# A hybrid Mamba, expert, attention and windowed-transformer layer on one core: GpSimd's difference in two halves, one clip over two PSUM banks, and other due times for the planner

## The chip, the cores and the metric

One core of a Trainium2 chip runs the whole program. The time is that of one execution on the device, in microseconds (us); a timing is the median of several runs. Engines are called as in the profile: PE (TensorE, with PEld for its weight loads), DVE (VectorE), ACT (ScalarE), POOL (GpSimd) and SP (SyncE, which issues DMAs). On-chip memory is SBUF; the results of matmuls land in PSUM, eight banks of 512 float32 for each of 128 partitions.

## The reference

The input x has 16 sequences of 256 tokens with 128 features, all in float32. Two blocks follow one another, and each adds two branches to its input:

```python
xn = layernorm(x)
x = x + mamba(xn) + experts(xn)            # selective scan, 256 channels, 16 states; top-1 of 8 experts, 512 hidden
xn = layernorm(x)
x = x + all_token_attention(xn) + windowed_transformer(xn)
```

The all-token attention has 16 heads of 8 features. Its weights are a power of an angle:

```python
q, k = l2norm(q), l2norm(k)
cos = einsum("bhsd,bhtd->bhst", q, k)
g = arccos(clip(cos, -1 + 1e-7, 1 - 1e-7))
score = (1 + g) ** (-3.2)
n_r, n_c = score.sum(-1), score.sum(-2)
k_tilde = score / n_r / n_c
probs = k_tilde / max(k_tilde.sum(-1), 1e-12)
out = (probs @ v) @ w_out.T + b_out
```

The windowed transformer has two layers of 8 heads of 64 features, each with normed and rotated queries and keys, a window of 64 tokens, and a gated feed-forward of width 341.

## The kernel before

The 16 sequences are worked in 8 pairs of 512 tokens. The work is cut into units, named by a letter and a step: `e_*` are the experts, `m_*` the Mamba branch of a pair (16 steps of a scan over 128x1024 elements), `f_*` the sum of the first block and the second layernorm, `g_*` the all-token attention, and `shift`, `qkv`, `heads`, `score` and so on the windowed layers. The branches of one pair depend on each other (attention of pair n needs `m_out` of pair n), but the scan of pair n+1 can overlap with the attention of pair n.

**The all-token attention of a pair** (`g_*`) has 8 blocks, one for each sequence b and four heads. For each block, m in the code:

1. `g_score`: twice, for two heads each, PE writes the cosines into two PSUM banks (L984), and DVE clips them into `cl`, one instruction of 128x512 for each bank (L1506). `cl` is a single buffer of 4 heads; DVE waits for the difference of the block before (`g_sub`), and each clip counts up `v_gs`.
2. `g_ln`: ACT writes ln(1 + c) into `la` (L1255) and ln(1 - c) over `cl` (L1257). 
3. `g_sub`: POOL forms the difference `la - cl` of 128x2048 elements in one instruction (L1726).
4. `g_tan`: Tanh (L1263) and Arctan (L1266), which give the angle; `g_pow`: Ln and Exp (L1273, L1275), which give the score.
5. `g_av`: DVE sums a block's columns (L1513) and scales the values, PE multiplies; `g_ev`, `g_avT`, `g_oT` and `g_out` finish; L1544 adds the attention of a pair to its input, L1549 the windowed layers.

`la` has two buffers, so two blocks are on their way together. ACT's functions lie in different tables, and a change of table is an instruction of its own (L758).

**Other work that the rows name.** A scan step is a product (L1428), a scan (L1434) and a product (L1440) on DVE, all of 128x1024 in SBUF; PE sums the states (L942); L1446 multiplies by the gate, at a pair's end. In the windowed layers POOL adds the rotated halves of queries and keys, 128x1024 (L1730); DVE takes a maximum over the sums of squares (L1572), scales by the norms (L1577), reduces scores over two banks for the softmax (L1587, L1588), and scales the output out of PSUM (L1601).

**The order.** A planner, run when the kernel is built, fixes the order of each engine's queue and the PSUM banks. `all_units` gives each unit a due time (`want`) and what it comes after; `schedule` walks through time, and each engine that is free takes the ready stage with the smallest due time, plus `SWITCH` if ACT would have to change its table. `STAGES` holds what a stage is taken to cost. Due times are a regular pattern (`EARLY`, `FIRST`, `SECOND`, `PERIOD`: the attention of pair i starts at EARLY + PERIOD x i, the Mamba branch of pair n from 2 on at FIRST + SECOND + 60 + PERIOD x (n - 2), and its step k stands 18 + k x (PERIOD - 30)/16 later), plus an offset for each kind of unit (`LATER`). On the chip each queue runs in that order, and semaphores hold an instruction until its inputs are there:

```python
cost = want[unit] + (SWITCH if needs and needs != table else 0)
if best is None or cost < best[0]:
    best = (cost, x, needs)
```

A unit that takes two banks got any two idle ones, except `score` of the windowed layers, whose two are neighbours, so that one instruction can read both.

## Time and profile before

| | |
|---|---|
| median of 3 runs | 2499.11 us (2494.23 to 2502.01) |
| the profiled execution | 2502.13 us, span 2500.8 us |
| busy in the span: PE, DVE, ACT, POOL | 1993.4, 1930.0, 1833.5, 525.0 us |
| mean granted clock of PE | 0.842 of full speed |
| instructions: PE, DVE, ACT, POOL | 10866, 3005, 2759, 206 |

The span runs from the first to the last instruction of the profiled execution; its time on the device is 1.3 us longer. Busy time is the sum of an engine's instructions; an instruction that is held up while it runs counts as busy for that long. The rows further down give groups of instructions (line, engine, operation, output and inputs, count), with their busy time, the mean of one in ns, and the idle time of the engine before them, with what ended it.

### The profile page before, as it was taken

To read this page: it belongs to the slowest core of one execution; us is meant where nothing else is said; L and a number is where in the kernel's file an instruction comes from. 1 tells how busy PE (TensorE), PEld (TensorE's weight loads), DVE (VectorE), ACT (ScalarE), POOL (GpSimd) and SP (SyncE) were. 2 spreads that over 40 slices of the span, in tenths; PEclk is the share of its full clock that TensorE was granted. 3 is DMA by queue.
4 is the path that set the end of the run, shared out by engine and by line. 5 is a ranking of instruction groups with operands and counts; after the bars stand their busy time and mean duration, and the time that the engine had idled before them with its cause. 6 is when DMAs were issued, how large, how long until landed. Compare 5 with 4: busy or idle time off the path is not lost.

```text
span 2500.8 us, 32678 instructions
## 1 busy us (share of the span) xinstructions
PE 1993.4 (80%) x10866; PEld 1328.3 (53%) x10866; DVE 1930.0 (77%) x3005; ACT 1833.5 (73%) x2759; POOL 525.0 (21%) x206
## 2 busy tenths in 40 slices
PE   4777778888678878878787888878787878888867
PEld 2544546775345555655465555655455555655645
DVE  5788895545997889699867889699968889674554
ACT  3436868697669677887777787887678786978883
POOL 2413121022112121302212121302112211221220
PEclk8787878999887888888787989888687989776778
DMA  7631112432211110111001110111001010000000
GB/s 250 222 98 56 51 34 67 131 116 85 83 42 53 46 35 18 40 35 55 22 13 48 39 48 13 40 46 53 13 31 39 32 53 1 1 1 5 1 1 5
DMA packets 67527, 126.29 MB, mean 51 GB/s; under 512 B 8836, under 2 KB 40132, under 8 KB 67236
## 3 DMA queue, kind: packets, MB, share of 16 engines
q1 hardware_dynamic: 61808, 113.19, 13.9%
q0 software_dynamic: 2816, 7.21, 0.8%
q10 hardware_dynamic: 2740, 3.80, 0.4%
q8 instruction: 92, 1.51, 0.2%
q14 instruction: 71, 0.58, 0.1%
HBM read 111.33 MB, written 12.85 MB: 50 GB/s over the span
## 4 chain that ended last, share of the span: by engine, by line
PE 31%; DVE 30%; ACT 18%; issue 16%; DMA 2%; SPq 1%; POOL 1%; DVEq 0%; ACTq 0%; POOLq 0%
PE ps L763 6%; DVE hB L1434 5%; PE ps L984 4%; PE ps L942 4%; DVE hB L1428 3%; DVE hB L1440 2%; PE ps L1068 2%; ACT arena L1255 2%; ACT arena L1331 2%; PE ps L1043 2%; DVE arena L1506 2%; DVE n_c L1513 2%; ACT L758 2%; PE ps L1103 2%; DVE lss L1568 2%
## 5 line engine op out<-in xcount | busy, mean ns | idle before, releaser
L1726 POOL TENSOR_TENSOR arena<-arena 128x2048 f32<-128x2048 f32 x64 | 297.5, 4649 | 1188.9 <-ACT arena L1257 1188.8
L763 PE MATMUL ps<-w_ident,arena 128*128 128x128 f32 x1647 | 301.1, 319 | 123.6 <-ACT arena L1331 43.7
L942 PE MATMUL ps<-hB,w_ident 128*128 128x512 f32 x512 | 303.4, 725 | 75.3 <-DVE hB L1440 75.2
L763 PEld LDWEIGHTS ps<-w_ident,arena 128*128 128x128 f32 x1647 | 227.7, 166 | 234.1 <-issue 139.1
L1434 DVE TENSOR_TENSOR_SCAN hB<-dA,hB 128x1024 f32<-128x1024 f32 x128 | 324.6, 2539 | 9.1 <-ACT dA L1219 8.8
L1730 POOL TENSOR_TENSOR arena<-arena,rb 128x1024 f32<-128x1024 f32 x64 | 151.9, 2374 | 574.6 <-DVE rb L1566 574.6
L1219 ACT ACTIVATE dA<-dtv,w_A_log 128x510 f32<-128x510 f32 x256 | 168.8, 718 | 109.6 <-DVE hB L1434 108.6
L1043 PE MATMUL ps<-w_l_wqkv,arena 128*128 128x512 f32 x384 | 212.5, 677 | 33.7 <-DVE lss L1568 15.5
L1506 DVE TENSOR_SCALAR arena<-ps 128x512 f32<-128x512 f32 x256 | 163.8, 681 | 63.6 <-PE ps L984 62.8
L1331 ACT ACTIVATE arena<-ps,nmx 128x128 f32<-128x128 f32 (+1 forms) x512 | 158.9, 397 | 65.5 <-DVE nmx L1588 64.8
L942 PEld LDWEIGHTS ps<-hB,w_ident 128*128 128x128 f32 x512 | 106.3, 229 | 181.9 <-issue 116.2
L1428 DVE TENSOR_TENSOR hB<-BC,du 128x1024 f32<-128x1024 f32 x128 | 180.4, 1414 | 28.6 <-PE ps L942 24.2
L984 PE MATMUL ps<-gqT,gkT 8*128 8x256 f32 x1024 | 176.3, 469 | 31.2 <-issue 12.4
L758 ACT ACT_TABLE_LOAD x142 | 182.2, 1283 | 15.3 <-issue 12.8
L1440 DVE TENSOR_TENSOR hB<-hB,BC 128x1024 f32<-128x1024 f32 x128 | 188.6, 1476 | 0.6
L1513 DVE TENSOR_REDUCE n_c<-arena 128x8 f32<-128x2048 f32 x64 | 145.8, 2278 | 31.6 <-ACT arena L1275 31.4
L1338 ACT ACTIVATE PT<-ps 128x384 f32<-128x384 f32 x256 | 124.3, 487 | 59.1 <-PE ps L763 42.3
L1255 ACT ACTIVATE arena<-arena,one_b 128x2048 f32<-128x2048 f32 x64 | 128.3, 2004 | 53.2 <-DVE arena L1506 45.2
L984 PEld LDWEIGHTS ps<-gqT,gkT 8*128 8x128 f32 x1024 | 106.5, 218 | 93.0 <-issue 81.2
L1068 PE MATMUL ps<-arena 64*128 64x128 f32 (+1 forms) x1024 | 154.9, 383 | 0.0
L1087 PEld LDWEIGHTS ps<-arena,PT 128*128 128x128 f32 x512 | 93.3, 218 | 113.7 <-ACT PT L1338 57.2
L1087 PE MATMUL ps<-arena,PT 128*128 128x65 f32 x512 | 107.2, 295 | 52.4 <-ACT PT L1338 43.9
(198 smaller groups left out, 4216.3 us busy)
## 6 DMA issues: line engine op xcount, KB each, us to landing
BC<-bc_d SPq DMA_DIRECT2D x128, 512.0 KB, 3.7
BC<-in_experts SPq DMA_DIRECT2D x31, 514.0 KB, 3.3
arena<-in_experts SPq DMA_DIRECT2D x15, 514.0 KB, 3.6
arena<-in_x SPq DMA_DIRECT2D x8, 256.0 KB, 5.8
xnT_d<-arena SPq DMA_DIRECT2D x8, 256.0 KB, 3.7
hB<-xnT_d SPq DMA_DIRECT2D x8, 256.0 KB, 2.6
x<-in_x SPq DMA_DIRECT2D x8, 256.0 KB, 2.9
out<-go SPq DMA_DIRECT2D x8, 256.0 KB, 2.3
```

The costliest lines, as they stand in the source:

```text
L758: a.preload_act_table_set(names[0])
L763: return t.transpose(out_, in_, ident[0:k, 0:k])
L942: e = t.matmul(lb(), ident, hB[k % 2][:, j], start=q == 0 and j == 0, stop=q == NQ - 1 and j == NG - 1)
L984: e = t.matmul(lb(z)[:, kt * L:(kt + 1) * L], gkT[32 * hi:32 * hi + GD, hb, kt * P:(kt + 1) * P], gqT[32 * hi:32 * hi + GD, hb], start=Tru ...
L1043: t.matmul(lb(), hT1[b][:, tt * P:(tt + 1) * P], w_lqkv[:, l, w * INNER:(w + 1) * INNER], start=True, stop=True).then_inc(p_q[b], 1)
L1068: e = t.matmul(o_, q_, kT[head_rows(z), k, b * L + j0:b * L + (L if qt else P)], start=False, stop=True)
L1331: e = a.activation(sm[b][:, hh, at], lb(z)[:, cols], ACT.Exp, bias=nmx[b][:, qt, hh:hh + 1])
L1428: v.tensor_tensor(hB[k % 2], Bb[q % 2], bc(du[:, c:c + 1], [P, NG, T]), ALU.mult).then_inc(v_bx, 1)
L1434: v.tensor_tensor_scan(hf, flat2(dA[k % 2]), hf, 0.0, ALU.mult, ALU.add).then_inc(v_scan, 1)
L1440: v.tensor_tensor(hB[k % 2], hB[k % 2], Cb[q % 2], ALU.mult).then_inc(v_hc, 1)
L1506: v.tensor_scalar(cl[:, 2 * (k % 2) + z], lb(z), -1.0 + 1e-7, 1.0 - 1e-7, ALU.max, ALU.min).then_inc(v_gs, 1)
L1726: g.tensor_tensor(la[m % 2], la[m % 2], cl, ALU.subtract).then_inc(g_sub, 1)
```

## The change

It has three parts.

- **The clip.** `g_score` takes two neighbouring banks, and one DVE instruction clips both, 128x1024 elements. It waits for the one half of the difference before it that reads the same part of `cl`; `v_gs` counts once for two banks.
- **The difference.** `g_sub` becomes two units a block, each one instruction on two heads (128x1024), each with a signal. Tanh waits for both halves; the next block's first pair of heads waits for the first half only.
- **The plan.** In the planner the clip is taken as 1.2 instead of 1.3, a difference as 2.4 instead of 4.6; `SWITCH`, `LATER` and the four numbers of the pattern have other values, and a new table, `STREAM`, shifts the due times of a whole branch of one pair. So each engine's queue has another order.

```diff
--- before.py
+++ after.py
@@ -64,8 +64,8 @@
     "m_fin": [("DVE", 1.5)], "x_load": [("SP", 0.1)], "m_out": [("PE", 2.1), ("DVE", 0.62)],
     "f_yg": [("POOL", 4.0)], "f_ln": [("DVE", 2.9), ("ACT", 0.6)], "f_xn": [("DVE", 1.1)], "f_tr": [("PE", 0.6), ("DVE", 0.7)],
     "g_qkv": [("PE", 0.86), ("DVE", 0.5)], "g_sq": [("ACT", 1.05), ("DVE", 1.5)], "g_norm": [("ACT", 0.7)],
-    "g_hd": [("DVE", 0.4), ("PE", 0.6), ("ACT", 0.5)], "g_score": [("PE", 1.3), ("DVE", 1.3)], "g_ln": [("ACT", 3.9)],
-    "g_sub": [("POOL", 4.6)], "g_tan": [("ACT", 3.8)], "g_pow": [("ACT", 3.9)], "g_av": [("DVE", 2.9), ("PE", 1.1)],
+    "g_hd": [("DVE", 0.4), ("PE", 0.6), ("ACT", 0.5)], "g_score": [("PE", 1.3), ("DVE", 1.2)], "g_ln": [("ACT", 3.9)],
+    "g_sub": [("POOL", 2.4)], "g_tan": [("ACT", 3.8)], "g_pow": [("ACT", 3.9)], "g_av": [("DVE", 2.9), ("PE", 1.1)],
     "g_ev": [("ACT", 0.5)], "g_avT": [("PE", 0.6), ("DVE", 1.15)], "g_oT": [("PE", 0.6), ("ACT", 0.5)],
     "g_out": [("PE", 1.2), ("DVE", 0.65)], "out": [("DVE", 0.65), ("SP", 0.1)], "zeros": [("DVE", 0.3)],
     "shift": [("PE", 0.4), ("ACT", 0.8)], "norm": [("DVE", 0.2), ("ACT", 0.5)], "qn": [("DVE", 1.25)], "heads": [("PE", 1.2), ("ACT", 1.0)],
@@ -79,14 +79,16 @@
 
 NEEDS = {"e_ln": "ln", "e_route": "ln", "m_weights": "ln", "m_dt": "ln", "m_ex": "ln", "f_ln": "ln", "g_norm": "ln", "g_ln": "ln", "g_pow": "ln",
          "norm": "ln", "score": "ln", "ln": "ln", "m_in": "silu", "g_tan": "tan", "gelu": "gelu"}
-SWITCH = 67.0
-
-LATER = {"down": 6, "f_ln": -5, "f_tr": 21, "f_xn": -15, "f_yg": -29, "g_av": 20, "g_avT": -6, "g_ev": 2, "g_hd": -38,
-         "g_ln": -22, "g_norm": -40, "g_oT": -1, "g_out": -13, "g_pow": 49, "g_score": -4, "g_sq": -18, "g_sub": -49,
-         "gelu": 57, "heads": 39, "hid": 4, "l_weights": 22, "ln": -31, "ln2": 29, "lnT": -27, "m_B": 56, "m_C": -54,
-         "m_bx": -16, "m_dt": 2, "m_du": -36, "m_ex": -7, "m_fin": 28, "m_hc": 8, "m_in": -88, "m_load": -3, "m_out": 20,
-         "m_scan": 21, "m_sum": -28, "m_weights": -1, "m_xp": -13, "norm": -31, "oT": 17, "on": 3, "out": -36, "pt": -3,
-         "pv": 54, "qkv": -6, "score": 3, "shift": 16, "wo": -9, "x_load": 18, "zeros": 50}
+SWITCH = 78.0
+
+LATER = {"down": 13, "f_ln": 28, "f_tr": -33, "f_xn": -25, "f_yg": 146, "g_av": 1, "g_ev": 10, "g_hd": -89, "g_ln": -13,
+         "g_norm": 26, "g_out": -5, "g_pow": 17, "g_qkv": -28, "g_score": -56, "g_sq": -4, "g_sub": 14, "g_tan": 6,
+         "gelu": -25, "hid": 10, "l_weights": -31, "ln": 41, "ln2": 11, "lnT": -84, "m_B": 132, "m_C": 11, "m_bx": 3,
+         "m_dt": 16, "m_du": -5, "m_ex": 53, "m_fin": 86, "m_hc": 136, "m_in": -23, "m_load": 14, "m_out": 5, "m_scan": -2,
+         "m_weights": -67, "m_xp": 29, "norm": -3, "on": 20, "out": -3, "pv": 13, "qkv": -4, "qn": -8, "score": -1, "up": 7,
+         "wo": 8, "x_load": 55, "zeros": -12}
+
+STREAM = {("g", 0): 1, ("g", 6): 1, ("g", 7): -8, ("l", 6): 1, ("l", 7): -7, ("m", 5): 2}
 
 LOADED = [15.0, 24.0]
 
@@ -111,13 +113,20 @@
     return STAGES[u]
 
 
+def stream(unit):
+    u, n, b, k = unit
+    if u in [x for x, _ in LAYER]:
+        return "l", n // LAY
+    return ("-" if u == "m_weights" else u[0][0]), n
+
+
 def all_units():
 
     want, after = {}, {}
 
     def unit(time, what, *comes_after):
         what = what + (0,) * (4 - len(what))
-        want[what] = time + LATER.get(what[0], 0.0)
+        want[what] = time + LATER.get(what[0], 0.0) + STREAM.get(stream(what), 0.0)
         after[what] = [x + (0,) * (4 - len(x)) for x in comes_after]
 
     for n in range(NPAIR):
@@ -182,7 +191,7 @@
              *[("f_tr", i - 2) for z in range(1) if i >= 2])
         unit(start - 20, ("f_ln", i), ("f_yg", i), ("m_out", i))
         unit(start - 20, ("f_xn", i), ("f_ln", i))
-        unit(start - 20, ("f_tr", i), ("f_xn", i), *[("g_sub", i - 1, 1, HB - 1) for z in range(1) if i])
+        unit(start - 20, ("f_tr", i), ("f_xn", i), *[("g_sub", i - 1, 1, 2 * HB - 2 + z) for z in range(2) if i])
         for tt in range(TT):
             unit(start, ("g_qkv", i, 0, tt), ("f_tr", i))
         unit(start, ("g_sq", i), *[("g_qkv", i, 0, tt) for tt in range(TT)])
@@ -198,14 +207,18 @@
                 t1 = start + 2 * cycle * b + cycle * (hb // 2)
                 z = hb % 2
                 m = HB * b + hb
-                prev = [("g_sub", i, *divmod(m - 1, HB))] if m else [("g_sub", i - 1, 1, HB - 1)] if i else []
+
+                p_ = (i, *divmod(m - 1, HB)) if m else (i - 1, 1, HB - 1)
+                prev = [[("g_sub", p_[0], p_[1], 2 * p_[2] + y)] if p_[0] >= 0 else [] for y in range(2)]
+                subs = [("g_sub", i, b, 2 * hb + y) for y in range(2)]
                 prev2 = [("g_av", i, *divmod(m - 2, HB))] if m >= 2 else [("g_av", i - 1, 1, HB - 2 + m)] if i else []
-                unit(t1, ("g_score", i, b, 2 * hb), *[("g_hd", i, b, k) for k in range(4)], *prev)
-                unit(t1, ("g_score", i, b, 2 * hb + 1), ("g_score", i, b, 2 * hb), *prev)
+                unit(t1, ("g_score", i, b, 2 * hb), *[("g_hd", i, b, k) for k in range(4)], *prev[0])
+                unit(t1, ("g_score", i, b, 2 * hb + 1), ("g_score", i, b, 2 * hb), *prev[1])
                 unit(t1, ("g_ln", i, b, hb), ("g_score", i, b, 2 * hb), ("g_score", i, b, 2 * hb + 1), *prev2)
-                unit(t1, ("g_sub", i, b, hb), ("g_ln", i, b, hb))
-
-                unit(t1 + 12, ("g_tan", i, b, hb), ("g_sub", i, b, hb), *[("g_sub", i, b, hb + 1) for x in range(1) if z == 0])
+                for y in range(2):
+                    unit(t1, subs[y], ("g_ln", i, b, hb))
+
+                unit(t1 + 12, ("g_tan", i, b, hb), *subs, *[("g_sub", i, b, 2 * hb + 3) for x in range(1) if z == 0])
                 unit(t1 + 20, ("g_pow", i, b, hb), ("g_tan", i, b, hb), *[("g_tan", i, b, hb + 1) for x in range(1) if z == 0])
                 unit(t1 + 20, ("g_av", i, b, hb), ("g_pow", i, b, hb), *prev2, *[("g_av", i, b, hb - 1) for x in range(1) if hb],
                      *[("g_ev", i, *divmod(m // 2 - 1, 2)) for x in range(1) if z == 0 and m], *[("g_ev", i - 1, 1, 1) for x in range(1) if m == 0 and i])
@@ -265,7 +278,7 @@
     return want, after
 
 
-EARLY, FIRST, SECOND, PERIOD = 49.0, 120.0, 105.0, 239.0
+EARLY, FIRST, SECOND, PERIOD = 120.0, 130.0, 80.0, 230.0
 
 
 def landed(unit):
@@ -370,7 +383,7 @@
 
     def choose(unit, count):
 
-        if unit[0] != "score":
+        if unit[0] not in ("score", "g_score"):
             return sorted(idle[0:count]) if len(idle) >= count else None
         pairs = [[z, z + 1] for z in range(7) if z in idle and z + 1 in idle]
         return min(pairs, key=lambda x: max(idle.index(z) for z in x)) if pairs else None
@@ -783,6 +796,10 @@
         def bank(unit, m=0):
             return ps[:, plan["banks"][bank_of(unit)][m]]
 
+        def two_banks(unit):
+            z0, z1 = plan["banks"][unit]
+            return ps[:, z0:z1 + 1:z1 - z0]
+
         before = shared_before(plan)
         all_first, all_wm, all_w = 16 * len(first), 16 * len(mamba), 16 * len(later)
 
@@ -985,7 +1002,7 @@
                                          gqT[32 * hi:32 * hi + GD, hb], start=True, stop=True)
                     e.then_inc(p_gs, 1)
                     for z in range(2):
-                        read_by(unit, v_gs, HB * m + 2 * (k % 2) + z + 1, z)
+                        read_by(unit, v_gs, 2 * m + k % 2 + 1, z)
                 elif u == "g_av":
                     m = BLOCKS * i + HB * b + k
                     if k % 2 == 0:
@@ -1248,7 +1265,7 @@
                     m = BLOCKS * i + HB * b + k
                     at, c_ = la[m % 2], cl
                     use(LN_EXP)
-                    a.wait_ge(v_gs, HB * (m + 1))
+                    a.wait_ge(v_gs, 2 * (m + 1))
                     if m >= 2:
                         a.wait_ge(p_av, m - 1)
                         a.wait_ge(v_vt, m - 1)
@@ -1259,7 +1276,7 @@
                     m = BLOCKS * i + HB * b + k
                     at = la[m % 2]
                     use(SIG, GELU, SILU)
-                    a.wait_ge(g_sub, m + 1)
+                    a.wait_ge(g_sub, 2 * (m + 1))
                     a.activation(at, at, ACT.Tanh, scale=0.25).then_inc(a_own, na.up())
                     use(SIG)
                     a.wait_ge(a_own, na.n)
@@ -1472,7 +1489,7 @@
                 elif u == "f_tr":
                     v.wait_ge(p_xT, i + 1)
                     if i:
-                        v.wait_ge(g_sub, BLOCKS * i)
+                        v.wait_ge(g_sub, 2 * BLOCKS * i)
                     v.tensor_copy(xnT, lb()).then_inc(v_xT, 1)
 
                 elif u == "g_qkv":
@@ -1500,10 +1517,10 @@
                 elif u == "g_score":
                     m, hb = BLOCKS * i + HB * b + k // 2, k // 2
                     if m:
-                        v.wait_ge(g_sub, m)
+                        v.wait_ge(g_sub, 2 * (m - 1) + k % 2 + 1)
                     v.wait_ge(p_gs, 2 * m + k % 2 + 1)
-                    for z in range(2):
-                        v.tensor_scalar(cl[:, 2 * (k % 2) + z], lb(z), -1.0 + 1e-7, 1.0 - 1e-7, ALU.max, ALU.min).then_inc(v_gs, 1)
+                    v.tensor_scalar(cl[:, 2 * (k % 2):2 * (k % 2) + 2], two_banks(unit), -1.0 + 1e-7, 1.0 - 1e-7,
+                                    ALU.max, ALU.min).then_inc(v_gs, 1)
                 elif u == "g_av":
                     m = BLOCKS * i + HB * b + k
                     hs = slice(k * HB, (k + 1) * HB)
@@ -1582,8 +1599,7 @@
                     if 4 * n + k >= 2:
                         v.wait_ge(a_e[b], 4 * n + k - 1)
                     hs = slice(2 * (k % 2), 2 * (k % 2) + 2)
-                    z0, z1 = plan["banks"][unit]
-                    both = ps[:, z0:z1 + 1:z1 - z0]
+                    both = two_banks(unit)
                     v.tensor_reduce(nmx[b][:, 0, hs], both[:, :, 0:P], AX.X, ALU.max, negate=True)
                     v.tensor_reduce(nmx[b][:, 1, hs], both[:, :, P:SC], AX.X, ALU.max, negate=True).then_inc(v_mx[b], 1)
                 elif u == "on":
@@ -1721,9 +1737,10 @@
                     for tt in range(TT):
                         g.indirect_dma_start(xn[i % 2][:, tt], None, y_d[q], bass.IndirectOffsetOnAxis(slot[:, TT * i + tt:TT * i + tt + 1], 0)).then_inc(d_yg[i % 2], 16)
                 elif u == "g_sub":
-                    m = BLOCKS * i + HB * b + k
+                    m = BLOCKS * i + HB * b + k // 2
+                    half = slice(2 * (k % 2), 2 * (k % 2) + 2)
                     g.wait_ge(a_ln, m + 1)
-                    g.tensor_tensor(la[m % 2], la[m % 2], cl, ALU.subtract).then_inc(g_sub, 1)
+                    g.tensor_tensor(la[m % 2][:, half], la[m % 2][:, half], cl[:, half], ALU.subtract).then_inc(g_sub, 1)
                 elif u == "qkv" and k % 3 == 1:
                     tt = 2 * b + k // 3
                     g.wait_ge(v_rot[b], 2 * (2 * n + k // 3 + 1))
```

## Rows read from the trace of the kernel before

**Rows 1.** The page: busy time and span share; the chain by engine and line.

```profile
PE 1993.4 (80%) x10866; PEld 1328.3 (53%) x10866; DVE 1930.0 (77%) x3005; ACT 1833.5 (73%) x2759; POOL 525.0 (21%) x206
...
PE 31%; DVE 30%; ACT 18%; issue 16%; DMA 2%; SPq 1%; POOL 1%; DVEq 0%; ACTq 0%; POOLq 0%
PE ps L763 6%; DVE hB L1434 5%; PE ps L984 4%; PE ps L942 4%; DVE hB L1428 3%; DVE hB L1440 2%; PE ps L1068 2%; ACT arena L1255 2%; ACT arena L1331 2%; PE ps L1043 2%; DVE arena L1506 2%; DVE n_c L1513 2%; ACT L758 2%; PE ps L1103 2%; DVE lss L1568 2%
```

**Rows 2.** Stretches: PE, PEld, DVE, ACT, POOL busy (instructions), clock, DMA share, GB/s.

```profile
625.00:2115.00 1490.00, 1206.21 (x6444) 778.12 (x6443) 1279.91 (x1830) 1144.25 (x1636) 301.08 (x101) 0.85 0.11 38
2115.00:2500.00 385.00, 311.75 (x1807) 223.11 (x1805) 214.99 (x429) 283.93 (x402) 79.25 (x24) 0.79 0.01 2
```

**Rows 3.** Groups of instructions on POOL: busy us, mean ns | idle before.

```profile
L1726 POOL TENSOR_TENSOR arena<-arena 128x2048 f32<-128x2048 f32 x64 | 297.5, 4649 | 1188.9 <-ACT arena L1257 1188.8
...
L1730 POOL TENSOR_TENSOR arena<-arena,rb 128x1024 f32<-128x1024 f32 x64 | 151.9, 2374 | 574.6 <-DVE rb L1566 574.6
```

**Rows 4.** Groups of instructions on DVE, same columns.

```profile
L1434 DVE TENSOR_TENSOR_SCAN hB<-dA,hB 128x1024 f32<-128x1024 f32 x128 | 324.6, 2539 | 9.1 <-ACT dA L1219 8.8
...
L1440 DVE TENSOR_TENSOR hB<-hB,BC 128x1024 f32<-128x1024 f32 x128 | 188.6, 1476 | 0.6
...
L1446 DVE TENSOR_TENSOR xs<-xs,zs 128x512 f32<-128x512 f32 x16 | 29.7, 1856 | 0.6
```

**Rows 5.** Single lines: duration ns min/median/max, first and last start us.

```profile
L1434 DVE TENSOR_TENSOR_SCAN hB<-dA,hB x128: 2258/2282/6550, 68.5 to 2099.7; 128x1024 f32<-128x1024 f32 x128
...
L1440 DVE TENSOR_TENSOR hB<-hB,BC x128: 1192/1217/5564, 76.5 to 2102.6; 128x1024 f32<-128x1024 f32 x128
...
L1446 DVE TENSOR_TENSOR xs<-xs,zs x16: 691/693/4844, 161.7 to 2112.0; 128x512 f32<-128x512 f32 x16
...
L1506 DVE TENSOR_SCALAR arena<-ps x256: 658/680/693, 206.5 to 2404.0; 128x512 f32<-128x512 f32 x128
```

**Rows 6.** Timeline of POOL and DVE: start us, us, instruction.

```profile
845.33 4.51 POOL L1726 TENSOR_TENSOR arena<-arena 128x2048 f32<-128x2048 f32 x1 [35.34 <-ACT arena L1257]
...
845.44 5.48 DVE L1440 TENSOR_TENSOR hB<-hB,BC 128x1024 f32<-128x1024 f32 x1
...
850.84 1.21 DVE L1428 TENSOR_TENSOR hB<-BC,du 128x1024 f32<-128x1024 f32 x1
...
997.05 0.56 DVE L1601 TENSOR_TENSOR arena<-ps,rs 128x384 f32<-128x384 f32 x1
```

**Rows 7.** Timeline of POOL: first and last of 40 differences that hold up DVE.

```profile
218.72 5.32 POOL L1726 TENSOR_TENSOR arena<-arena 128x2048 f32<-128x2048 f32 x1 [1.64 <-ACT arena L1257]
...
2390.39 4.50 POOL L1726 TENSOR_TENSOR arena<-arena 128x2048 f32<-128x2048 f32 x1 [4.79 <-ACT arena L1257]
```

**Rows 8.** Chain that ended last: first and last of 45 held-up pieces.

```profile
219.59 4.50 DVE lss L1572
...
2390.73 5.25 DVE arena L1577
```

**Rows 9.** Groups on DVE: the clips and the reductions over two banks.

```profile
L1506 DVE TENSOR_SCALAR arena<-ps 128x512 f32<-128x512 f32 x256 | 163.8, 681 | 63.6 <-PE ps L984 62.8 <-POOL arena L1726 0.4 <-issue 0.2
...
L1588 DVE TENSOR_REDUCE nmx<-ps 128x2 f32<-128x384 f32 x128 | 70.0, 547 | 0.0
...
L1587 DVE TENSOR_REDUCE nmx<-ps 128x2 f32<-128x256 f32 x128 | 53.4, 417 | 78.4 <-PE ps L1068 78.1
```

**Rows 10.** Waits for the clips: us in total, times, longest us.

```profile
ACT arena L1255 <- DVE arena L1506: 45.2, 28, 4.7
...
PE ps L984 <- DVE arena L1506: 11.8, 10, 2.4
```

**Rows 11.** Timeline of DVE: the attention results of pairs 4 to 6.

```profile
1682.80 0.68 DVE L1544 TENSOR_TENSOR go<-ps,x 128x512 f32<-128x512 f32 x1
...
1980.09 0.66 DVE L1544 TENSOR_TENSOR go<-ps,x 128x512 f32<-128x512 f32 x1
...
2224.64 0.69 DVE L1544 TENSOR_TENSOR go<-ps,x 128x512 f32<-128x512 f32 x1
```

## The prediction

> **What bounds the kernel now.** I read the page first: busy shares and the composition of the chain that ended last, then the stages, then single groups of instructions. The reader is to see that no engine is full: TensorE is busy for 80% of the span, VectorE for 77%, ScalarE for 73%, GpSimd for 21%, and the chain is shared by TensorE (31%), VectorE (30%), ScalarE (18%) and issue (16%) [rows 1]. So the order in which the three queues meet sets the time, and a microsecond taken from one engine gives back a part of itself. The stages differ [rows 2]: from 625 to 2115 us, where scans and attention overlap, VectorE is busy for 1280 of 1490 us (86%); from 2115 us to the end no scan runs and it falls to 56%. GpSimd's long instruction is the difference of the logarithms, 64 times 4.65 us [rows 3].
>
> The rows then show something that no share shows. VectorE's scan takes 2282 ns in the median, but 2539 in the mean and 6550 at most; the multiplication behind it 1217 and 1476, the product with the gate 693 and 1856 [rows 4, 5]. The timeline says when: the long ones overlap GpSimd. At 845.33 GpSimd begins a difference of 4.51 us, at 845.44 VectorE begins a multiplication that takes 5.48 us instead of 1.22, and ends 1.1 us after GpSimd [rows 6]. I matched every VectorE instruction that is over 0.15 us above its group's median with the GpSimd instruction running then: 40 of the 64 differences hold up a VectorE instruction (the first at 218.72, the last at 2390.39 us [rows 7]), 123 us together, and 31 of the 64 rotary additions hold one up for 47 us more; 170 us in all. Held up are instructions with two inputs in SBUF, and a few with one, as the maximum over the sums of squares at 219.59 [rows 8]; the clips, which read PSUM, stay between 658 and 693 ns [rows 5]. Where those instructions stand in the chain of waits I counted 113 of the 170 us, 81 of them under the differences, in 45 pieces from the 4.50 us at 219.59 to the 5.25 us at 2390.73 [rows 8].
>
> The Trainium skill (SBUF — State Buffer, section Who interferes with whom) says that VectorE and GpSimd share one port pair, that the one that starts first keeps it for its whole instruction, and that the other is blocked. The trace agrees: one 4.26 us block at 845.44, ending with GpSimd's instruction.
>
> **The change, part by part.**
>
> *The clip.* 128 pairs of instructions at 681 ns each [rows 9] become 128 instructions over two banks. The trace has no such clip; it has reductions over two banks, 417 ns for 256 elements and 547 for 384 [rows 9], a slope of 1.0 ns an element and no visible price for the second bank. 1024 elements then take 547 + 640 = 1190 ns; no saving would be 1362. I take 1200, since the other VectorE instructions of 1024 elements have a median of 1217 [rows 5]: 0.16 x 128 = 20 us of VectorE. The clips are 2% of the chain, 50 us [rows 1], so 50 x 0.16/1.36 = 6 us of the end (bounds 0 and 20). What it costs: the first bank of a pair comes free some 0.5 us later. TensorE's score matmuls waited 10 times for a clip, 11.8 us in all [rows 10]; 10 x 0.5 = 5 us at worst, taken as 0, since Ln waits for both clips anyway (28 times [rows 10]) and gets both 0.16 us earlier.
>
> *The difference in halves.* On GpSimd 64 x 4.65 us become 128 at the price of the rotary addition, the same operation on 128x1024: 2.37 us [rows 3], so 4.75 us for each block, 6 us more in all on an engine that is idle for 79%. Hidden. The earlier signal lets the next block's first clips begin 2.3 us sooner. VectorE's clips waited 0.4 us for a difference in the whole span [rows 9], so the signal by itself gives nothing; its worth is only the planner's freedom. No new wait is added. Behind a second half that has to let a VectorE instruction pass stand only the rotary additions; Tanh, which waits for both halves, would come 1.2 to 2.3 us later, and is covered by the other work that the plan puts ahead of it, or else costs that much 64 times at most.
>
> What the halves do give is a shorter hold. A VectorE instruction that comes x us into a difference now stands for 4.5 - x; with halves it stands for 2.4 - x or, in the second half, for 4.7 - x. I replayed the 64 differences on the recorded VectorE queue. Undivided, the replay gives 108 us of stalls (recorded: 123). In halves it gives 50 us if the held instruction, and one that follows it at once, pass before the second half. If the second half takes the port right behind the first held instruction and holds the next one, the total stays at 108. So between 0 and 58 us of VectorE are saved. I take 35, nearer the good end, because instructions that read PSUM, as the scaling at 997.05 [rows 6], often follow the held one, and the second half runs under them unseen. Of that, 81/123 lies on the chain: 23 us; and since other chains are close behind (no engine above 80%), I let 60% through: 14 us (bounds 0 and 38).
>
> A page's rule gives the other sum. The Trainium skill (the same page and section) holds that the order of issue decides who blocks, whatever the shape. By that alone two short instructions are two chances to block, and the sum is the 0 us end of these bounds.
>
> *The plan.* All due times change; each engine's queue is another permutation. The trace can't show the new queues. It shows what order alone is worth: the attention results of three pairs are added up at 1682.80, 1980.09 and 2224.64 us [rows 11], so two cycles of nearly the same work take 297 and 245 us. A swing of some 20 us a cycle, over five such cycles in which swings partly cancel, is 20 x the root of 5 = about 45 us either way. Below nothing too: a plan can be worse. I take -10, because the planner now counts the short clip and the short difference, which it could not use before, and because the new numbers leave the last pair's attention where it was (49 + 7 x 239 = 1722 before, 120 + 7 x 230 - 8 = 1722 after, on the planner's clock) while cycles are spaced 9 closer.
>
> Sum: 6 + 14 + 10 = 30 us. The profiled execution took 2502.1 us (span 2500.8), so 2472; it stands 3 us above the median of the runs, 2499.1, so **2469 us**, 1.2% faster.
>
> **The rivals.**
>
> *The halves do not help.* The second half takes the port behind the first held instruction and the stalls stay near 123 us; the order is about even. For it: in the long stage VectorE is busy for 86%, so the next instruction with two SBUF inputs is rarely far (at 850.84 a multiplication follows directly on the held one [rows 6]). Against it: after a held instruction the port may just as well go to VectorE's next. It leaves the clip: 2499 - 6 = 2493 us, at the edge of no change.
>
> *The order loses more than the edits give.* Its place is the end of the last scans. Before, the last multiplication behind a scan is due at 1480 + 18 + 196 + 8 = 1702 on the planner's clock; after, at 1420 + 18 + 187.5 + 136 = 1761.5, while the last pair's attention stays at 1722. 60 units are, at 2501 us for 1961 units (49 + 8 x 239), 76 us. The last scan now starts at 2099.7 us [rows 5] and the last stage takes 385 us [rows 2]; the last pair can't enter attention before. If half of the slip stays, the end moves by 38 and the edits give 20 back: 2499 + 18 = 2517; if all stays, 2555. I take 2525. It decides from a slip of 20 us that the last stage can't absorb. Against it: the scan itself becomes due 91 units earlier (1715 to 1624), a due time only ranks what is ready, and in the last stage VectorE has 44% idle to absorb work.
>
> *The order gains much more*: the long stage's idle time shrinks by one more good cycle, 40 us: 2430 us.
>
> **How the numbers follow.** The forecast (2440 to 2491, its own range) has 0.55, the large gain 0.07; no help 0.14; the order that loses 0.24. A measurement of this kernel can't tell less than about 0.3% (7.5 us) from no change. Faster, below 2491.6: 0.62; same: 0.15; slower, above 2506.6: 0.23. From 2430 to 2522 leaves out about half of the large gain (0.05) and half of the losing order (0.13).
>
> **What would show it.** Clips: 128 instructions of 128x1024 at about 1.2 us; 1.36 would refute the first term. GpSimd: 128 differences near 2.35 us. The scan's longest should fall from 6.55 to about 4.6 us and its mean from 2539 to about 2400 ns, the gate product's mean (1856) most of all; an unchanged mean is the first rival. The stalls together should be about 135 us. The order: the cycles between results, 245 and 297 us now [rows 11], and where the last scan stands: past 2120 us with a last stage still near 385 us is the losing order.  Wrong I would be above all through the order, which I can't see.

## The result, and the profile after

The changed kernel took 2515.5 us (median of 4 runs, 2506.7 to 2519.6) beside 2498.8 us before: 1.0061 times as long, with an interval of [1.0037, 1.0084]. It was forecast to be 1.2% faster; it is 0.6% slower. The profiled execution is the shortest of the four, with a span of 2505.4 us.

The page of the changed kernel: busy time, then the chain. It answers to [rows 1]. The changed kernel's lines stand 13 to 17 lower than before: L1726 is now L1743, L1434 is L1451, L1506 is L1522.

```profile
PE 2004.3 (80%) x10866; PEld 1342.5 (54%) x10866; DVE 1917.1 (77%) x2877; ACT 1831.2 (73%) x2753; POOL 591.6 (24%) x270
...
PE 39%; DVE 27%; issue 15%; ACT 15%; DMA 3%; SPq 1%; POOL 1%; DVEq 0%; ACTq 0%; POOLq 0%
```

The reader is to see that VectorE and ScalarE are busy for less than before (13 and 2 us), TensorE and GpSimd for more (11 and 67 us), and that the time rose. TensorE's share of the chain went from 31% to 39%; its mean granted clock is 0.836 beside 0.842. The groups of instructions of the changed kernel (answering to [rows 3, 4, 9]):

```profile
L1743 POOL TENSOR_TENSOR arena<-arena 128x1024 f32<-128x1024 f32 x128 | 344.5, 2711 | 1000.8 <-ACT arena L1274 1000.8
L1451 DVE TENSOR_TENSOR_SCAN hB<-dA,hB 128x1024 f32<-128x1024 f32 x128 | 329.3, 2574 | 4.0 <-ACT dA L1236 3.5
...
L1522 DVE TENSOR_SCALAR arena<-ps 128x1024 f32<-128x1024 f32 x128 | 155.7, 1216 | 56.3 <-PE ps L1001 55.7
```

The clip over two banks takes 1216 ns, as forecast. But the busy time of all clips fell from 163.8 to 155.7 us only, 8 us and not 20: 256 x 681 ns is 174 us, more than the 163.8 us in which VectorE was busy with them, since the second of two clips in a row begins some 0.08 us before the first ends. The mean of an instruction counts that overlap twice.

The scan's mean did not fall (2574 ns, 2539 before). Its longest did, from 6.55 to 4.46 us. The mean of the gate product, of which the prediction expected most, fell from 1856 to 747 ns, its longest from 4844 to 1574. Scans are held for a shorter time each, but 24 of them are held where 15 were. Single lines of the changed kernel, duration in ns min/median/max (answering to [rows 5]):

```profile
L1451 DVE TENSOR_TENSOR_SCAN hB<-dA,hB x128: 2257/2282/4456, 64.7 to 2124.9; 128x1024 f32<-128x1024 f32 x128
...
L1463 DVE TENSOR_TENSOR xs<-xs,zs x16: 691/692/1574, 157.8 to 2132.1; 128x512 f32<-128x512 f32 x16
```

The timeline of the changed kernel, GpSimd and then VectorE, shows how two halves hold two instructions (start us, duration us):

```profile
818.72 7.07 POOL L1743 TENSOR_TENSOR arena<-arena 128x1024 f32<-128x1024 f32 x2 [0.51 <-ACT arena L1274]
```

```profile
820.18 3.47 DVE L1451 TENSOR_TENSOR_SCAN hB<-dA,hB 128x1024 f32<-128x1024 f32 x1
823.58 2.25 DVE L1589 TENSOR_SCALAR lss<-lss 128x32 f32<-128x32 f32 x1
825.74 0.18 DVE L1613 RECIPROCAL rs<-ps 128x6 f32<-128x6 f32 x1
```

The first half holds the scan up by 1.2 us (3.47 instead of 2.28). When it ends, VectorE's scan runs first and GpSimd's second half waits, so that both halves together last 7.07 us instead of 4.7. Then the second half takes the port at once and holds the next VectorE instruction, a tiny one of 0.17 us, for 2.1 us. In 23 of the 64 blocks both halves held an instruction and the second half itself took over 2.6 us. Counted as in the prediction, VectorE stood for 118 us under the differences and 43 under the rotary additions, 161 us in all; before, it was 123 + 47 = 170.

### The profile page after: what moved, and what is told of

Its sections match the earlier page's. It is cut to its first block, busy times and chain, and to the rows that moved or that the text cites. A ratio compares the mean times of both kernels' runs of the same rounds, so it can differ in the third digit from the quotient of the medians.

```text
span 2505.4 us, 32609 instructions
## 1 busy us (share of the span) xinstructions
PE 2004.3 (80%) x10866; PEld 1342.5 (54%) x10866; DVE 1917.1 (77%) x2877; ACT 1831.2 (73%) x2753; POOL 591.6 (24%) x270
## 4 chain that ended last, share of the span: by engine, by line
PE 39%; DVE 27%; issue 15%; ACT 15%; DMA 3%; SPq 1%; POOL 1%; DVEq 0%; ACTq 0%; POOLq 0%
PE ps L776 7%; PE ps L959 6%; PE ps L1001 4%; DVE hB L1451 4%; PE ps L1060 3%; PE ps L1085 3%; DVE hB L1445 3%; DVE hB L1457 3%; PE ps L1120 2%; ACT L771 2%; DVE arena L1522 2%; DVE rb L1583 2%; PE ps L1151 2%; ACT arena L1348 2%; DVE lss L1585 1%
## 5 line engine op out<-in xcount | busy, mean ns | idle before, releaser
L1743 POOL TENSOR_TENSOR arena<-arena 128x1024 f32<-128x1024 f32 x128 | 344.5, 2711 | 1000.8 <-ACT arena L1274 1000.8
L776 PE MATMUL ps<-w_ident,arena 128*128 128x128 f32 x1647 | 315.2, 332 | 148.2 <-DVE arena L1594 38.9
L776 PEld LDWEIGHTS ps<-w_ident,arena 128*128 128x128 f32 x1647 | 239.7, 173 | 263.6 <-issue 183.1
L1451 DVE TENSOR_TENSOR_SCAN hB<-dA,hB 128x1024 f32<-128x1024 f32 x128 | 329.3, 2574 | 4.0 <-ACT dA L1236 3.5
L959 PE MATMUL ps<-hB,w_ident 128*128 128x512 f32 x512 | 295.5, 709 | 44.9 <-DVE hB L1457 44.5
L1001 PE MATMUL ps<-gqT,gkT 8*128 8x256 f32 x1024 | 184.2, 486 | 40.0 <-DVE arena L1522 18.8
L1522 DVE TENSOR_SCALAR arena<-ps 128x1024 f32<-128x1024 f32 x128 | 155.7, 1216 | 56.3 <-PE ps L1001 55.7
L1457 DVE TENSOR_TENSOR hB<-hB,BC 128x1024 f32<-128x1024 f32 x128 | 176.9, 1393 | 0.3
L1085 PE MATMUL ps<-arena 64*128 64x128 f32 (+1 forms) x1024 | 160.5, 395 | 0.0
L1319 ACT ACTIVATE sq<-ps 128x512 f32<-128x512 f32 x128 | 76.3, 596 | 104.9 <-DVE lss L1585 77.4
```

The lines of the kernel that those rows point to most:

```text
L776: return t.transpose(out_, in_, ident[0:k, 0:k])
L959: e = t.matmul(lb(), ident, hB[k % 2][:, j], start=q == 0 and j == 0, stop=q == NQ - 1 and j == NG - 1)
L1001: e = t.matmul(lb(z)[:, kt * L:(kt + 1) * L], gkT[32 * hi:32 * hi + GD, hb, kt * P:(kt + 1) * P], gqT[32 * hi:32 * hi + GD, hb], start=Tru ...
L1085: e = t.matmul(o_, q_, kT[head_rows(z), k, b * L + j0:b * L + (L if qt else P)], start=False, stop=True)
L1451: v.tensor_tensor_scan(hf, flat2(dA[k % 2]), hf, 0.0, ALU.mult, ALU.add).then_inc(v_scan, 1)
L1457: v.tensor_tensor(hB[k % 2], hB[k % 2], Cb[q % 2], ALU.mult).then_inc(v_hc, 1)
```

## The experiments

"Old order" below means the queues of the kernel before, every unit on every engine in its old place; "new order" means those of the changed kernel. "Stalls" is the time by which VectorE's instructions exceed their group's median while GpSimd works, counted instruction by instruction as in the prediction (over 0.15 us each). Some expectations below name stalls up to 9 us higher than this count. Ratios are against the kernel before on the same chip, which took 2502.2 us for the first four runs of the table, 2502.1, 2498.2 and 2495.9 us for the next fours; runs on different chips are compared by their ratios.

| run | median us | ratio, interval | stalls us |
|---|---|---|---|
| kernel before | 2498.8 | 1 | 170 |
| changed kernel | 2515.5 | 1.0061 [1.0037, 1.0084] | 161 |
| old_order_halves | 2474.3 | 0.9896 [0.9864, 0.9927] | 146 |
| old_order_pairs | 2516.7 | 1.0056 [1.0038, 1.0075] | 171 |
| old_order_both | 2489.8 | 0.9946 [0.9925, 0.9967] | 143 |
| new_order_old_ops | 2537.5 | 1.0137 [1.0106, 1.0168] | 185 |
| new_order_halves | 2521.2 | 1.0080 [1.0055, 1.0105] | 160 |
| old_order_halves_late | 2477.7 | 0.9888 [0.9864, 0.9911] | 148 |
| old_order_quarters | 2462.0 | 0.9837 [0.9816, 0.9858] | 125 |
| old_order_halves_rotary | 2453.2 | 0.9815 [0.9793, 0.9838] | 134 |
| new_order_free_banks | 2516.8 | 1.0066 [1.0045, 1.0088] | 166 |
| new_code_old_numbers | 2508.3 | 1.0040 [1.0022, 1.0058] | 138 |
| old_order_quarters_rotary | 2422.0 | 0.9678 [0.9651, 0.9704] | 104 |
| old_order_short_difference | 2387.6 | 0.9542 [0.9516, 0.9568] | 45 |
| new_order_short_difference | 2389.9 | 0.9581 [0.9555, 0.9607] | 34 |
| new_order_quarters_rotary | 2458.4 | 0.9860 [0.9837, 0.9883] | 119 |
| old_order_memsets | 2390.2 | 0.9582 [0.9562, 0.9602] | 56 |
| old_order_eighths_rotary | 2421.0 | 0.9710 [0.9688, 0.9731] | 71 |

**Order against edits.** Four kernels separate the queues from the instructions.

*old_order_halves*, in the kernel before:

```diff
-g.tensor_tensor(la[m % 2], la[m % 2], cl, ALU.subtract).then_inc(g_sub, 1)
+for y in range(2):
+    part = slice(2 * y, 2 * y + 2)
+    g.tensor_tensor(la[m % 2][:, part], la[m % 2][:, part], cl[:, part], ALU.subtract).then_inc(g_sub, 1)
```

with the waits of the change for the single halves.

> The order and the banks of the kernel before, the difference in two halves, the clips as before. Theory 'the order loses': the halves are worth little by themselves, 2490 to 2500 us; single stalls of VectorE end at 2.4 us instead of 4.7, but the second half holds up another instruction, and the stalls together stay over 130 us of 170. Theory 'the halves lose' (more instructions on GpSimd, each taking the port again): 2508 us or more. Theory of the prediction: stalls near 135 us and 2485 us.

2474.3 us, 1.0% faster, with 146 us of stalls: no theory had given the halves that much, the prediction's 2485 us came nearest.

*old_order_pairs*: one replay of the planner with the old queues fixed, in which a score unit takes neighbours where there are any, and in which the choice among idle banks is partly drawn by a seeded random number (its code is left out here).

```diff
-plan = schedule()
+plan = schedule(schedule())   # the second pass keeps each queue and hands out the banks anew
```

> The queues of the kernel before, clips and difference as before, only the PSUM banks handed out anew so that 112 of the 128 score units get two neighbouring banks. A control: if banks matter little, within 0.3% of 2499 us. If the need for neighbours is what costs time (other units wait longer for a bank), 2508 us or more.

2516.7 us: this other assignment of banks, with every queue and every instruction the same, costs 0.6%. It is one draw; whether the need for neighbours or the draw costs the time, the run can't tell.

*old_order_both*: the same banks, the halves, and the clip of the change for the 112 pairs that are neighbours.

> As the run with neighbouring banks, and both edits: one clip for 112 of 128 pairs (two clips for the other 16), the difference in halves. The order theory: 2485 to 2497 us, that is the edits gain up to 0.5% and all that was lost in the changed kernel was lost by its order. The theory that the edits lose: 2510 us, as in the changed kernel.

2489.8 us, 1.1% below its control with the same banks. The halves alone gave 1.0%, so the clip adds nothing that can be measured.

*new_order_old_ops*, in the changed kernel:

```diff
-v.tensor_scalar(cl[:, 2 * (k % 2):2 * (k % 2) + 2], two_banks(unit), -1.0 + 1e-7, 1.0 - 1e-7, ALU.max, ALU.min).then_inc(v_gs, 1)
+for z in range(2):
+    v.tensor_scalar(cl[:, 2 * (k % 2) + z], lb(z), -1.0 + 1e-7, 1.0 - 1e-7, ALU.max, ALU.min).then_inc(v_gs, 1)
...
-g.tensor_tensor(la[m % 2][:, half], la[m % 2][:, half], cl[:, half], ALU.subtract).then_inc(g_sub, 1)
+g.tensor_tensor(la[m % 2], la[m % 2], cl, ALU.subtract).then_inc(g_sub, 1)   # for the first of two units only
```

with the waits and counts of the kernel before.

> The order and the banks of the changed kernel, with neither edit: two clips for each pair, one whole difference, issued where the first half stood. The order theory: as slow as the changed kernel or slower, 2512 to 2525 us. The theory that the edits lose: 2500 us or less.

2537.5 us, slower than the range of either theory: the new order, its banks included, costs 1.4%, and the edits give back 0.8% (1.0061 to 1.0137). Its last scan begins at 2147 us, 47 later than in the kernel before, and what follows takes 13 us less; the loss is made before the last stage. The last scan of the fifth pair still begins at 1239 us, 18 earlier than before (1257); the scans of the last three pairs then take 65 us more (908 beside 843).

**What the halves gain by.**

*new_order_halves*: the new order with the halves and two clips.

> The order and banks of the changed kernel with the difference in halves, but two clips for each pair of banks. Isolates the one clip: by the count of instructions (256 x 681 ns against 128 x 1216) it should be some 6 us slower than the changed kernel, 2520 us; by the busy time of the clips as the profile shows it (163.8 against 155.7 us, since two clips in a row overlap by some 0.1 us) within 3 us of it, 2513 to 2518 us.

2521.2 us, ratio 1.0080 beside 1.0061 with the one clip; the intervals overlap. The clip is worth between nothing and some 5 us. Beside *new_order_old_ops* (1.0137) the halves alone give 14 us in this order, with 160 us of stalls instead of 185.

*old_order_halves_late*:

```diff
-v.wait_ge(g_sub, 2 * (m - 1) + k % 2 + 1)
+v.wait_ge(g_sub, 2 * m)
```

> The order of the kernel before with the difference in halves, but each clip waits for both halves of the block before, as it did for the whole. If the gain of the halves is the shorter hold of the port, the time stays at 2474 us (2466 to 2482). If it is the earlier signal, it goes back to 2495 to 2500.

2477.7 us, ratio 0.9888 beside 0.9896: the earlier signal is worth nothing that can be measured; the gain comes with the division of the instruction itself.

*old_order_quarters* has `range(4)` and pieces of one head; *old_order_halves_rotary* cuts the rotary addition too:

```diff
-g.tensor_tensor(qkr[:, tt], qkr[:, tt], rb, ALU.add).then_inc(g_rb[b], 1)
+for w in range(2):
+    e = g.tensor_tensor(qkr[:, tt, w], qkr[:, tt, w], rb[:, w], ALU.add)
+e.then_inc(g_rb[b], 1)
```

> The order of the kernel before, the difference in four parts of 128x512. By the theory of the hold, the longest single stall falls to 1.3 us and the sum of the stalls under the differences from 99 to 70 or 80 us: 2455 to 2470 us. If the total hold decides and not the length of a piece: 2474 us again.

> The order of the kernel before, the difference in halves, and the rotary addition in two halves of 128x512 as well, with one signal at the end. By the theory of the hold its stalls (49 us) fall by about 15 us and the time to 2462 to 2472 us; otherwise 2474 us.

2462.0 and 2453.2 us. Both went the way of the theory of the hold; the second fell 9 us below its expected range, by more than its stalls account for (12 us of stalls, 21 of time).

*old_order_quarters_rotary* has both:

> The order of the kernel before, the difference in quarters, the rotary addition in halves. By the theory of the hold both gains add up: 2474 - 12 (quarters) - 21 (rotary) = 2441 us, 2430 to 2455. If the gains come from the luck of one order against small shifts, anything from 2440 to 2475.

2422.0 us, 8 us below its expected range, 3.2% faster than the kernel before and the fastest version with the whole computation, together with the next. Single line of that run:

```profile
L1434 DVE TENSOR_TENSOR_SCAN hB<-dA,hB x128: 2257/2284/3367, 68.6 to 2026.1; 128x1024 f32<-128x1024 f32 x128
```

*old_order_eighths_rotary* has pieces of 128x256:

> The order of the kernel before, the difference in eight parts of 128x256, the rotary addition in four of 128x256. By the theory of the hold: another 20 to 25 us of stalls less than with quarters and halves (105), 2395 to 2410 us. If starts of instructions and re-taking of the port eat it up, 2420 us.

2421.0 us: the stalls fell by another 33 us and the time did not. That is the expectation's second branch (2420 us); the theory of the hold alone had 2395 to 2410. The groups on GpSimd with quarters and with eighths:

```profile
L1728 POOL TENSOR_TENSOR arena<-arena 128x512 f32<-128x512 f32 x256 | 396.5, 1579 | 1072.6 <-ACT arena L1257 1072.5
```

```profile
L1729 POOL TENSOR_TENSOR arena<-arena 128x256 f32<-128x256 f32 x512 | 488.5, 989 | 982.4 <-ACT arena L1257 982.3
```

GpSimd needs 7.6 us for a block in eighths, 6.2 in quarters and 4.65 undivided: pieces wait for the VectorE instructions that pass, so the difference itself comes later. In the run with eighths Tanh on ScalarE waits for a difference 9 times, 23.9 us in all and at most 4.2, where in the kernel before and in *old_order_halves* it waited for none, and in *old_order_quarters* once, for 1.7 us; and GpSimd's share of the chain is 6% instead of 1%.

```profile
ACT arena L1263 <- POOL arena L1729: 23.9, 9, 4.2
```

```profile
PE 28%; DVE 25%; ACT 22%; issue 15%; POOL 6%; DMA 2%; SPq 1%; DVEq 0%; ACTq 0%; POOLq 0%
```

That this lateness ate the gain fits these waits; no run takes it away by itself.

**The whole price of the hold.** *old_order_short_difference* and *new_order_short_difference* leave out the subtraction for 504 of 512 columns of each head, the second in the new order with two clips:

```diff
-g.tensor_tensor(la[m % 2], la[m % 2], cl, ALU.subtract).then_inc(g_sub, 1)
+g.tensor_tensor(la[m % 2][:, :, 0:8], la[m % 2][:, :, 0:8], cl[:, :, 0:8], ALU.subtract).then_inc(g_sub, 1)
```

> The order of the kernel before; the difference is formed on 8 of 512 columns of each head only, and the rest of the subtraction is left out. It prices the whole hold of the port by the differences: 123 us of stalls go. At the rate of the halves (28 us of time for 22 us of stalls) that is more than 100 us: 2390 to 2410 us. If other work bounds the kernel soon after, it flattens: 2430 to 2445 us.

2387.6 us, just below its range: the differences, on an engine that is busy for 21%, cost 4.6% of the time.

*old_order_memsets* gives GpSimd nearly the same length of work, nearly all of which writes but does not read; most of the subtraction is left out here too:

```diff
+for y in range(HB):
+    g.memset(la[m % 2][:, y, 8:], 0.0)
+    e = g.memset(cl[:, y, 8:], 0.0)
+e.then_inc(g_sub, 1)
```

> The order of the kernel before, the difference on 8 of 512 columns of each head, and behind it eight memsets of 128x504 over the rest of the two tiles before the signal is given; most of the subtraction is left out. GpSimd is busy about as long as with the whole difference (some 4.5 us), but reads almost nothing from SBUF. If it is GpSimd's reading that holds VectorE up, stalls stay near 45 us and the time at 2388 to 2400 us. If any work of GpSimd holds it up, or if the late signal costs the time, 2450 us or more.

2390.2 us. Its groups on GpSimd:

```profile
L1728 POOL MEMSET arena<- 128x504 f32 x256 | 132.6, 518 | 0.0
L1729 POOL MEMSET arena<- 128x504 f32 x256 | 132.5, 518 | 0.0
...
L1726 POOL TENSOR_TENSOR arena<-arena 128x32 f32<-128x32 f32 x64 | 28.4, 443 | 1143.3 <-ACT arena L1257 1143.2
```

Memsets in a row overlap a little, so the three groups are not to be added up: GpSimd is busy for 491.3 us in all beside 525.0 before, which leaves some 264 us for them where the whole differences took 297.5. So GpSimd's time and its late signal cost little: 3 us between the medians, 0.4% (10 us) between the ratios. What costs is that it reads SBUF while VectorE wants its second input. The memsets are also short pieces, but that is not what spares VectorE: 35 of its scans and multiplications with both inputs in SBUF ran beside them, for 51 us, and none took over 0.1 us more than its median. Seven instructions with a single tensor input in SBUF, all `tensor_scalar`, did stand beside the memsets, 10 us together: VectorE's maximum over the sums of squares took up to 2.9 us instead of 0.17. The Trainium skill (SBUF — State Buffer, section Who interferes with whom) states both: a VectorE instruction with two inputs in SBUF contends with a GpSimd instruction that reads SBUF and not with one that only writes it, while a `tensor_scalar` can enter a two-port mode, in which VectorE contends with GpSimd. The trace agrees with both; which mode the seven ran in, it does not show.

**Why the new order is slower.**

*new_order_free_banks*: the new queues, fixed in a second pass of the planner as above, with any idle banks for a score unit; halves, two clips.

> The queues of the changed kernel, the difference in halves, two clips, but the PSUM banks handed out without the rule that a score unit takes neighbours. Against 2521 us with the rule (the run new_order_halves). If the rule makes the new order slow, as handing banks out anew under the old order cost 14 us: 2500 to 2510 us. If the order of the queues does it: 2515 to 2530 us.

2516.8 us, ratio 1.0066 beside 1.0080 with the rule: the rule is not what slows the new order. This too is one draw of banks.

*new_code_old_numbers*:

```diff
-SWITCH = 78.0
+SWITCH = 67.0
...
-EARLY, FIRST, SECOND, PERIOD = 120.0, 130.0, 80.0, 230.0
+EARLY, FIRST, SECOND, PERIOD = 49.0, 120.0, 105.0, 239.0
```

and `LATER` as before, `STREAM` empty.

> The changed kernel with the numbers of the plan before: switch, offsets, pattern, and no shifts of branches. The shorter costs, the two units a block and the neighbouring banks stay, so the planner makes a third order. If the new numbers are at fault, near the old order with both edits, 2475 to 2495 us. If any order not chosen for its own structure is worse, 2510 to 2560 us.

2508.3 us: with the old numbers the new structure gives a third order, 1.4% above the old order with the halves (2474.3 us), though its stalls (138 us) are fewer. The new numbers are not alone at fault.

> The order and banks of the changed kernel, two clips, the difference formed on 8 of 512 columns of each head and otherwise left out, as in old_order_short_difference (2388 us). If the new order is slower because its queues meet the port's hold more often (151 against 123 us under the differences), most of the gap of 35 us goes: 2385 to 2405 us. If the order is slower by itself, the gap stays: 2415 to 2430 us.

> The order and banks of the changed kernel, two clips, the difference in quarters and the rotary addition in halves; the old order takes 2422 us with them. If the port's hold makes the gap: 2430 to 2445 us. If the order is slower by itself: 2450 to 2470 us, that is 35 or more above.

2389.9 us with the short difference, within 0.4% of the old order's 2387.6 by the ratios: the gap is nearly gone without the whole difference. It was 1.4% with the whole difference and 1.9% with halves and two clips (1.0080 beside 0.9896). With quarters and the halved addition it is 2458.4 beside 2422.0 us, 1.9% by the ratios. The groups of the scan in the new order, first with the whole difference, then with the short one:

```profile
L1451 DVE TENSOR_TENSOR_SCAN hB<-dA,hB 128x1024 f32<-128x1024 f32 x128 | 324.3, 2535 | 4.0 <-ACT dA L1236 3.5
```

```profile
L1451 DVE TENSOR_TENSOR_SCAN hB<-dA,hB 128x1024 f32<-128x1024 f32 x128 | 303.0, 2369 | 6.9 <-ACT dA L1236 6.3
```

So both orders are about equally good without the whole difference, and the new one loses more by it. How it loses more stays open. The late signal of the difference is at most a part: in *new_order_old_ops* VectorE's clips waited for it for 7.5 us and Tanh never, and in *new_order_halves*, where the gap is wider, neither waited. At one for one, the sum of the stalls explains 15 of the 35 us with the whole difference (185 against 170), and 14 or 15 of some 46 with halves (160 against 146) and with quarters (119 against 104). Nor do the stalls that stand in the chain that ended last explain it: 123 against 111 us, 91 against 87, and 59 against 49. TensorE's granted clock is lower in the new order in each of these comparisons (0.835 against 0.842, 0.837 against 0.850, 0.847 against 0.864), but also with the short difference (0.857 against 0.871), where the times are nearly equal; whether it is a cause or goes along, no run separates.

## Why the prediction was wrong

- **The order** is the step that failed. The text took -10 us from a range of 45 us either way; by *new_order_old_ops* it was +35 (1.4%). The reason given, that the planner now counts the shorter clip and difference, was no evidence on the order's worth: the planner knows nothing of the shared port, and what the new queues lost is nearly gone without the whole difference. The other reason, that the last pair's attention keeps its place, left out the offsets of its units: that of `g_score` went from -4 to -56, that of `g_pow` from 49 to 17.
- **The rival that came true** is "the order loses more than the edits give", close in its numbers (2525 us taken, 2515.5 measured), its mechanism in part. It had the last scan slip by 38 to 76 us. With the old instructions the slip was 47 us, and the last stage took back 13; in the changed kernel the last scan began at 2124.9 us, 25 later, and what followed took 21 us less. But the rival derived the slip from the due times alone, and with the short difference the same queues slip by 15 us only (2008.3 beside 1993.4).
- **The halves** were the right mechanism. VectorE's stalls fell by 24 us in the old order and 25 in the new one (forecast 35), and the time by 14 us in the new order (forecast 14) and by 26 in the old one. That the forecast was met in the new order, to within the intervals of some 7 us, owes something to luck: the stalls saved were fewer, and a microsecond of them gave more than the prediction let through (81/123 on the chain, then 60%), in the old order about a whole one. From 170 us of stalls to 45 in the old order the time falls by 111 us; single steps lie on either side of that rate.
- **The first rival**, no help from the halves, was half right: in some blocks the second half does take the port right behind the first held instruction, its sign, an unchanged scan mean, came, and the stalls under the differences are 118 us. But in the same order with whole differences they are 142. It was wrong to conclude that nothing is gained.
- **The clip**: 1216 ns was right (1200), the saving of 20 us of busy time wrong (8), because the product of mean and count ignores the overlap of neighbours. At the end it gave nothing measurable (forecast 6 us). In the old order, banks handed out anew so as to have neighbours cost 14 us.
- **The signal** by itself gives nothing: right. GpSimd's own time was wrong, 47 us more (344.5 beside 297.5) instead of 6, since halves that wait for VectorE count as busy; in the changed kernel Tanh waited for none of them, so that it was hidden, as forecast.

## What to carry to other kernels

Where GpSimd reads SBUF beside VectorE instructions with two inputs there, look at VectorE's maximum against its median: an idle-looking GpSimd can cost several per cent. Cut its instructions into pieces (here down to about 1.3 us), and test the edit with every queue and every bank left as it was before a new plan is searched: 3.2% were there, and the new plan hid them. A planner that does not know a shared port can hand back by chance what an edit wins.

## What was not expected of the hardware

- A VectorE instruction that has been held up mostly runs before GpSimd's next piece (7.07 us for two halves at 818.72), and that piece then holds VectorE's next one. So cutting shortens most stalls (the scan's longest is 4.3 us above its median with the whole difference, 2.2 with halves, 1.1 with quarters and halved additions) but lowers the sum more slowly: 170, 146, 104 us.
- It is no cap. In *old_order_halves*, *old_order_quarters* and *old_order_eighths_rotary*, two multiplications by the norms (L1577) each stood through all pieces of a block, 4.4 to 5.4 us over their median of 1.2. In the run with eighths, one of them and the first piece began together at 1810.95 us; the eight pieces ran to their end in 5.50 us, and the multiplication took 6.58. What decides who goes next, no run shows.

```profile
1810.95 5.50 POOL L1729 TENSOR_TENSOR arena<-arena 128x256 f32<-128x256 f32 x8
1810.95 7.72 DVE L1577 TENSOR_TENSOR arena<-arena,lss 128x1024 f32<-128x1024 f32 x2 [1.97 <-ACT lss L1313]
```

- Leaving out the differences removes 125 us of stalls and 111 us of time, about 0.9 us each, though VectorE is busy for only 77%. Not all of that need be VectorE's time: TensorE's granted clock rose from 0.842 to 0.871, and the same 10866 matmuls kept it busy for 1931.8 us instead of 1993.4. No run separates the two.
- Memsets of nearly the same length cost little: 2390.2 us beside 2387.6.
- Another assignment of PSUM banks alone, with nothing else changed, moved the time by 0.6% (one draw).
